# A gated delta recurrence on one core: the turned solve in the value convolution's tile, the next turn's K side inside this turn, and a new order

## The reference, cut to what matters

```
q = silu(conv(h @ Wq.T)); k = silu(conv(h @ Wk.T)); v = silu(conv(h @ Wv.T))
k = k / max(norm(k), 1e-12)
alpha, beta = sigmoid(h @ Wa.T + ba), sigmoid(h @ Wb.T + bb)
def step(S, kt, vt, qt, at, bt):
    v_old = S @ kt
    S = clip(at * S + bt * outer(vt - at * v_old, kt), -5, 5)
    return S, S @ qt
g = silu(h @ Wg.T + bg);  out = (y * g) @ Wo.T
```

## Time and profile before

| | us |
|---|---|
| median of three runs | 1870.27 |
| lowest, highest | 1864.04, 1873.93 |
| span of the profiled execution (first to last instruction) | 1869.6 |
| start of the turns to the first state of the last turn | 57.5 to 1171 |
| the last turn's chain, gates and bound | 1171 to 1246 |
| attention output and mixture of experts | 1246 to 1870 |

### The profile page before, as it was taken

One profiled execution on the slowest core, in us unless ns is written; L12 is line 12 of the kernel. 1 busy time (PEld: TensorE's weight loads), 2 busy tenths in 40 slices (PEclk: granted clock), 3 DMA queues, 4 the chain that ended last, 5 costly groups with the idle time before them and its releaser, 6 DMA issues. The chain is left out here.

```text
span 1869.6 us, 59680 instructions
## 1 busy us (share of the span) xinstructions
PE 1620.9 (87%) x24736; PEld 1142.6 (61%) x24736; DVE 1389.8 (74%) x1892; ACT 895.2 (48%) x1768; POOL 1127.0 (60%) x1362
## 2 busy tenths in 40 slices
PE   7778999999988989999988988835999848999997
PEld 4445666666666656566656666625888836666664
DVE  8777888888898888898898887447787664444443
ACT  5745555555655655655556555313444232222221
POOL 0657768768767767768777768017343103666664
PEclk9989989989999999989999988977999859999998
DMA  5221231231231231231231230246333163455543
GB/s 184 49 53 25 69 91 37 67 93 37 67 92 37 67 93 36 67 93 36 69 92 36 65 75 26 69 144 227 135 128 110 46 230 79 94 93 100 96 91 51
DMA packets 89465, 156.59 MB, mean 84 GB/s; under 512 B 15708, under 2 KB 54116, under 8 KB 88108
## 3 DMA queue, kind: packets, MB, share of 16 engines
q1 hardware_dynamic: 73292, 124.80, 22.6%
q0 software_dynamic: 15904, 27.93, 8.1%
HBM read 112.56 MB, written 40.12 MB: 82 GB/s over the span
## 5 line engine op out<-in xcount | busy, mean ns | idle before, releaser
L1386 PE MATMUL d_ps<-hT,turn_shared 128*128 128x512 f32 x768 | 402.8, 632 | 8.4 <-DVE d_Vp L1171 4.6
L953 POOL TENSOR_TENSOR turn_shared<-turn_shared,d_tmp 128x31 f32<-128x31 f32 (+15 forms) x496 | 289.7, 584 | 38.9
L948 POOL TENSOR_TENSOR d_tmp<-turn_shared 128x31 f32<-128x31 f32 (+15 forms) x496 | 286.4, 577 | 38.9
L1024 DVE SCALAR_TENSOR_TENSOR turn_shared<-d_ps,d_cw,turn_shared 128x1023 f32<-128x1023 f32 (+2 forms) x192 | 245.3, 1278 | 15.0 <-ACT turn_shared L682 12.6
L742 ACT ACTIVATE d_S<-d_S,gamma_chunk 128x64 f32<-128x64 f32 x448 | 130.9, 340 | 184.5 <-DVE d_S L1052 144.6
L2539 POOL DMA_INDIRECT m_xt<-rows_scratch,m_slot_i x71 | 70.2, 989 | 183.3 <-DVE m_slot_i L2632 95.7
L1386 PEld LDWEIGHTS d_ps<-hT,turn_shared 128*128 128x128 f32 x768 | 126.8, 192 | 87.6 <-issue 71.4
L2526 ACT ACTIVATE m_hm<-m_ps,m_b_tile 128x128 f32<-128x128 f32 x284 | 80.9, 368 | 206.3 <-PE m_ps L2706 206.3
L122 PE MATMUL o_po<-wo_split,y_high 128*128 128x256 f32 x512 | 101.7, 302 | 44.8 <-DVE y_low L115 44.8
L2549 POOL DMA_INDIRECT out<-m_yo,m_slot_i x71 | 114.2, 1608 | 41.2 <-issue 20.3
L2696 PE MATMUL m_ps<-m_w,m_xs 128*128 x284 | 136.2, 602 | 1.6 <-DVE m_xs L2641 1.0
(11 more groups left out here) (251 smaller groups left out, 3737.2 us busy)
## 6 DMA issues: line engine op xcount, KB each, us to landing
turn_shared<-steps_scratch SPq DMA_DIRECT2D x64, 256.0 KB, 4.2
d_qg<-gamma_scratch SPq DMA_DIRECT2D x64, 256.0 KB, 5.0
y_scratch<-d_yT SPq DMA_DIRECT2D x256, 64.0 KB, 1.8
d_arow<-ab_scratch SPq DMA_DIRECT2D x128, 128.0 KB, 3.1
y<-y_scratch SPq DMA_DIRECT2D x8, 2048.0 KB, 8.7
m_w<-w_in SPq DMA_DIRECT2D x16, 512.0 KB, 10.0
turn_shared<-x_by_half_in SPq DMA_DIRECT2D x8, 512.0 KB, 6.8
rows_scratch<-gates SPq DMA_DIRECT2D x4, 1024.0 KB, 11.6
```

Source lines behind the costliest of these rows:

```text
L948: nc.gpsimd.tensor_tensor(tv, Tq[:, s + 1:, s].rearrange("p (r a) -> p r a", a=1).broadcast_to([P, left, known]), X[:, s, 0:known].rearran ...
L953: nc.gpsimd.tensor_tensor(X[:, s + 1:, 0:known], X[:, s + 1:, 0:known], tv, ALU.subtract).then_inc(s_sub, 1)
L1024: nc.vector.scalar_tensor_tensor(out=dst[:, j + 1:], in0=src[:, 0:T - 1 - j], scalar=cw[:, u // BP % 2, n, 2 - j:3 - j], in1=dst[:, j + 1: ...
L1386: return nc.tensor.matmul(dst[:, g, :], w[:, m % 2, n, dc, :], hT[:, dc, at:at + G], start=(dc == 0), stop=(dc == DC - 1))
```

## The change

1. `XT` moves from `Tq` to the memory of `v_made`. `turn_matrix` drops its waits for `cross_second` and `keep_x`; `turn_x` waits for both value silus of its turn, and `first_v` of the next turn for `cross_second`.
2. `norms` and `scalars` of the next turn move into this iteration, behind `turn_matrix`; so does `join`. POOL clears X before the bound terms of the iteration, and decays the last quarter of K after the solve.
3. The waits for the PSUM pairs are new, with the order: `proj_q` waits for `keep_w` in every turn (before, the solve matrix), `v_turned(0)` for the solve matrix, `v_turned(1)` for `bound_max`, `z_turned(0)` for the q taps, `z_turned(1)` for `scale_v`, `proj_v(1)` also for `bound_max`, `kk` for the K taps.
4. The order of each engine is written anew, as one list of calls for an iteration. The instructions are the same in kind and number.

```
-        P1, XT = Xn, Tq
+        P1, XT = Xn, v_made[:].rearrange("p (a b) -> p a b", b=CH)
...
             def turn_matrix(u):
                 dve.wait_ge(s_tc, u + 1)
-                if u:
-                    dve.wait_ge(s_xp, 2 * u)
-                    dve.wait_ge(s_xz, u)
...
             def turn_x(u):
                 dve.wait_ge(s_sub, 62 * (u + 1))
+                dve.wait_ge(s_qsilu, 4 * u + 4)
...
             def first_v(u, b2):
                 elif u:
                     act.wait_ge(s_qsilu, 4 * u)
+                    act.wait_ge(s_xp, 2 * u)
...
             def proj_q(u, b2, i):
                     if b2 == 0:
-                        if u == 1:
-                            pe.wait_ge(s_wt, 1)
+                        if u:
+                            pe.wait_ge(s_wt, 2 * u - 1)
...
             def v_turned(u, hf):
                 if hf == 0:
-                    if u >= 2:
-                        pe.wait_ge(s_mx, 2 * u - 3)
+                    if u + 1 < TURNS:
+                        pe.wait_ge(s_tt, 2 * u + 4)
...
                 else:
-                    if u + 1 < TURNS:
-                        pe.wait_ge(s_tt, 2 * u + 4)
-                    elif u >= 2:
+                    if u <= 1:
+                        pe.wait_ge(s_V, 2 * u + 1)
+                    else:
                         pe.wait_ge(s_mx, 2 * u - 2)
```

More of the change, by code:

```diff
@@ L953, in substitute, with solve @@
                 nc.gpsimd.tensor_tensor(X[:, s + 1:, 0:known], X[:, s + 1:, 0:known], tv, ALU.subtract).then_inc(s_sub, 1)
-            def solve(u):
-                scale_rows(u)
-                for row in range(CH - 1):
+            def solve(u, rows):
+                for row in rows:
+                    if row == 0:
+                        scale_rows(u)
                     substitute(u, row)
@@ L995, in _ @@
             clear_x(0)
-            solve(0)
+            solve(0, range(CH - 1))
             gamma_k(0)
@@ new lines, in _ @@
+                if it == TURNS:
+                    split_input(0)
+                if chain:
+                    state(tc, 2)
+                if prep:
+                    tap_v(u, 0, 0)
+                if it == TURNS:
+                    split_weights(0)
+                if prep:
+                    tap_v(u, 0, 1)
+                if chain:
+                    state(tc, 3)
+                if prep:
+                    tap_v(u, 0, 2)
+                if bound:
+                    bound_scan(tb, 0)
@@ new lines, in _ @@
+                if chain:
+                    state(tc, 4)
+                if bound:
+                    bound_max(tb, 0)
+                if prep:
+                    attention(u, 0)
+                if chain:
+                    state(tc, 5)
+                    turn_y(tc, 0)
+                if it == TURNS:
+                    split_weights(1)
+                if prep:
+                    decayed_q(u)
+                if chain:
+                    update_max(tc, 0)
+                    state(tc, 6)
@@ new lines, in _ @@
+                if prep:
+                    attention(u, 1)
+                    turn_norm(u)
+                if new_k:
+                    decay(un, 0)
+                if it == TURNS:
+                    split_weights(2)
+                if prep:
+                    tap_v(u, 1, 0)
+                    tap_v(u, 1, 1)
+                if chain:
+                    state(tc, 7)
+                    update_max(tc, 1)
+                if prep:
+                    tap_v(u, 1, 2)
+                if new_k:
+                    tap_k(un, 0, 0)
@@ new lines, in _ @@
+                if it == TURNS:
+                    split_weights(3)
+                if new_k:
+                    tap_k(un, 1, 1)
+                if chain:
+                    state(tc, 11)
+                if new_k:
+                    tap_k(un, 1, 2)
+                if it == TURNS:
+                    split_input(1)
+                if new_k:
+                    decay(un, 1)
+                if chain:
+                    state(tc, 12)
+                if prep:
+                    largest_k(u)
@@ new lines, in _ @@
+                if new_k:
+                    solve_matrix(un, 0)
+                    solve_matrix(un, 1)
+                if chain:
+                    state(tc, 13)
+                    turn_y(tc, 2)
+                if prep:
+                    scale_v(u, 0)
+                if new_k:
+                    turn_matrix(un)
+                if chain:
+                    state(tc, 14)
+                if new_k:
+                    norms(un)
+                    scalars(un)
+                if bound:
+                    bound_scan(tb, 1)
@@ L1753, in _ @@
             kk(1, 1)
+            v_turned(0, 0)
             w_product(0, 0)
```

800 lines of the change are left out of this document (423 added, 377 removed).

## The result

The changed kernel takes **1935.2 us** (median of 4 runs, 1930.5 to 1936.0), the kernel before 1869.2 us (4 runs); the ratio is 1.036, 95% interval 1.034 to 1.038. The forecast was 1882 us with a range up to 1905, so it fell outside. One of the four executions of the first kernel of experiment 5 ran slow (2886 us, at a granted clock of 0.62) and is left out of that kernel's number. The profiled execution of the changed kernel spans 1934.3 us, 64.7 more than before.

What follows compares the result with a forecast made beforehand. No engine is full; POOL's ring and DVE's and PE's ring are nearly equally long, at 70.0 us a turn. Turns +8, turn 1 -2, gates +2, clock +4 sum to +12, 1882 us; range 1840 to 1905.

Steps and rivals of the forecast that it cites:

- the removed wait is worth nothing: Turned solve matrix: its dropped waits gain nothing, since DVE's own queue holds the transpose.
- POOL has cover: POOL in the new turn: solve done at 66.65 us, with 4 us of cover.
- section 2: State 14 to DVE's first value tap, 21.0 to 43.25 us into the turn: PE and ACT set the pace.
- section 3: First value tap to the next turning of X: DVE sets the pace, 25.65 us and waits of 1.85, ending at 70.6.
- turn 1: The turn without bound work: POOL's floor comes first, about 69 us instead of 71.1, -2.
- the walk: The new turn followed by each engine's order with earlier durations: 70.6 us against 70.0, +0.6 a turn, +8 over thirteen turns.
- section 1: DVE's turning of X to state 14: DVE sets the pace, state 14 starts at 21.0 us, PE has some 17 of work.
- the clock's size and place: PE's half clock in the new order: bounds 0 to +2 us a turn, 0.3 taken, +4; costly only if reaching section 2.
- The third rival: Half clock reaches section 2, seen under the q projections: +2 to +3 us a turn, 1907 us, chance 0.17.
- the edge, "+2" for the turn with the gates: Last chain: gates begin behind step 7 instead of the second state, 54 to 56 us, +2.
- edges that cancel: Ends of the recurrence: -2 us for turn 1 and +2 for the turn with the gates.

Runs made afterwards that it cites:

- experiment 5: First kernel: the changed kernel filled with added PE products at two places, two of them replaced by 32 products of 64 x 64: 1945.8 us, ratio 1.043.
- experiment 1: The kernel before in its own order, with only the memory part of the change: 1868.3 us against 1866.3, ratio 1.001.
- experiment 6: Cross products replaced by eight large products of zeros: 1880.7 us in the changed kernel filled at the head of section 3, 1867.9 in the kernel before.
- experiment 4: The changed kernel with a burst of 2048 cross products (32 x 32), without waits, added behind the recurrence: the burst takes 116.1 us.
- experiment 2: The changed kernel with four added PE products of 256 columns a turn in two gaps at the head of section 3: 1916.4 us, ratio 1.026.
- experiment 3: The changed kernel filled at the head of section 3, with three more added PE products a turn in section 1: 1937.5 us, ratio 1.039.
- the mixed burst: The changed kernel with 2048 cross products at its end and one product of 256 columns after every 16: the burst takes some 220 us without any pause.

## Why the prediction was wrong, step by step

- **Right: the removed wait is worth nothing** (experiment 1); POOL has cover (X is turned 3.5 us and more after the solve's end in the undisturbed turns); section 2 is paced by PE and ACT, with its first q projection behind ACT's copy of W (1.14 us of wait, walked at 1), and takes 22.5 us on average (walked 22.25); section 3 is 27.3 in an undisturbed turn (27.35); turn 1 falls by 2.3 us (68.8 between the clears, forecast -2). The turn of experiment 6, 20.4 + 22.5 + 27.3 = 70.2 us, has no cross products but shows how long the rest takes nearly undisturbed: within 0.4 of the walk's 70.6. By that the new order would have gained nothing even so.
- **Failed: section 1, "PE has only some 17 us of work in this section".** PE was busy for 18.8 us of it and stood still for 2.0 more at the ends of blocks of instructions, a cost that the walk puts at nothing; section 1 took 22.4 us instead of 21.0, +1.4 a turn (+2.0 against the 20.4 of experiment 6). The pauses are shown to be instruction supply (experiment 4); how the excess divides between them and the half clock of 5.7 us a turn stays open. The order before has the same instructions at about the same pace in its dense stretch, so why a pause costs more in the new order, among hand-overs that PE, ACT and DVE wait for, is my reading and not shown. The wait of 0.92 us with no releaser in the earlier trace rows is no such pause: no packet of instructions landed in the 4.9 us before it.
- **Failed: the clock's size and place.** I took 0.3 a turn, near the lower of my bounds, 0 and 2. There is no more half clock than before, but it lies elsewhere: it cost 1.3 a turn at the head of section 3 (experiment 2: 17 us in all) and a part of section 1. The third rival had the mechanism and the sum (+2 to +3 a turn), but its test looked at the wrong place: under the first q projection the clock was 1.00 (section 2 above), and the fall came some 23 us later (668.3 against 645.1), where new gaps of 1.3 and 1.2 us lie in front of a chain over three engines. I had walked these gaps as "a product of K and q that stands behind ACT's copy of K" and put only their length into the sum.
- **Failed: the edge, "+2" for the turn with the gates.** I compared the length of the last chain before and after, and never asked when it starts. My own walk had the answer: the first W product stands behind state 14, over 21 us after the turning of X, where before it was 12.0 (749.68 less 737.64 in the earlier trace rows). What a pipeline delays inside a turn it pays once more at the end: +12.3, of which a part, not measured by itself, is the half clock there.
- **Two slips in the numbers.** The third rival's own terms, 2.6 by 13 on 1870 with edges that cancel, give 1904, not 1907; and a range that ends at 1905 cuts that rival in the middle and does not take in most of it.

Together: the turns +49 instead of +10, the end +12 instead of +2, and 3.5 around them.

## What to carry to other kernels

Count instructions beside microseconds: where an order packs many small products together, compare their number with what PE can be given (here 256 in 3.6 us), and look for idle time without a releaser that ends behind a packet of the instruction queue. Where a gap is put in front of a hand-over across engines, price that hand-over at half clock too. And when an order shifts one pipeline against another inside the loop, add the shift once at the end.

## What the runs showed of the hardware

- PE's instructions come in blocks of 256 (a packet of 16384 bytes), one every 3.5 to 4.0 us in the burst; in the turns such pauses at the ends of blocks were up to 3.2 us long (experiment 3). In the time line they stand as idle time with no releaser, ending 1.2 to 1.75 us after a packet of the instruction queue landed. The number of packets is that of PE's instructions by 256: 130 and 130.0, 108 and 108.2.
- In the mixed burst PE was busy, as the profile counts it (the ends of products are modelled), for all of 80 us, and for 220 in all, at a granted clock of 0.50, while streams of 64 x 64 products and projections in the turns run at 1.00 (the rows of section 2). The Trainium skill, "TensorE: Matmul & The Clock Gate", section What's actually happening, says that activity releases the throttle; that run doesn't agree. Whether the 32 x 32 products are the reason was not tried.
